# Halves of the expert weights made two tiles ahead, and unread products in bursts of eight, in a float32 Mamba-2 and mixture-of-experts block

## The chip, the core and the metric

The kernel runs on one core of a Trainium2 chip. The metric is the device time of one execution in microseconds (us), the median of several runs. Engines are named as the profile names them: PE is TensorE's matmul side and PEld its weight loads, DVE is VectorE, ACT is ScalarE, POOL is GpSimd, SP is SyncE, which here only starts DMAs.

## The reference

The input is 4 sequences of 512 tokens with 256 features in float32, so 2048 tokens. A modulated layer norm feeds a Mamba-2 style attention part (64 heads), whose result is added to the input. A second modulated layer norm feeds a mixture of experts, whose result is added again. The part that matters here is the routed experts:

```python
probs = softmax(x @ gate_w.T)                    # 64 experts
topk_w, topk_idx = top_k(probs, 6)               # 6 experts per token
topk_w = topk_w / sum(topk_w)
h = silu(einsum('th,eih->tei', x, experts_w1))   # inner size 176
y = einsum('tei,ehi->teh', h, experts_w2)
routed_out = einsum('teh,te->th', y, combine)
```

The reference computes all experts for all tokens and keeps six of them. The kernel computes only the pairs that were chosen.

## The kernel before

The program has four stages: the attention part, the second norm with routing, the two shared experts, and the routed experts. During routing each token's row is sent by indirect DMA into a region of its expert in the DRAM tensor `grouped`. The routed work is then a list of ETILES = 160 tiles of 128 rows (2048 * 6 / 128 + 64); each tile has one expert, and the tables `owner_no` and `first_row` in SBUF give its number and its first row. Tiles beyond the used ones run on a spare row region. After the last tile a stage of 16 groups (`got`, lines 386 and 1291 on) gathers six rows per token, scales them with the token's shares and adds them to the result.

Every float32 product is made of three products of halves: `split_mm` (lines 400 to 402) multiplies high by high, high by low and low by high. The high half is a rounded copy made by ScalarE (`high`, line 718) in the type fp32r, the low half is the difference, made by VectorE (`low`, line 888). Both helpers serve many tiles, so the rows are told apart by the tile they write.

For tile i of the expert loop:

- SP loads 128 rows (`load_rows`, line 348, into `x_rows`, 12 buffers) and the expert's two weight matrices (`load_weights`, lines 337 and 339, into `ew`, DEEP = 4 buffers of 128 x 864). `load_weights(i)` waits until `w_lo` of tile i-4 has been made, which frees the buffer. Before every fourth tile `four` reads the next four row and expert numbers into SP's registers. Then SP issues, in this order: rows n, rows n+1, weights n, rows n+2, weights n+1, rows n+3, weights n+2, weights n+3.
- TensorE turns the rows with two transposes (`turn`, line 657) into `p_x`, two buffers. ScalarE makes `xe_hi` (in the trace `hw_hi`, 128x256) and VectorE `xe_lo` (`hw_lo`), both in `rows_in`.
- ScalarE makes `ew_hi` in `weights`, VectorE `ew_lo` in `weights_low`, 128x864 each. `weights(i)` waits for the load and for `second_mm` of tile i-4, `weights_low(i)` for `w_hi` of the same tile.
- `first` (twelve products of 128x128 with 88-column weights) waits for `w_lo` and `x_lo` of its tile and for `hid_silu` of tile i-2. ScalarE makes `hid` with Silu (line 876, `hid_rows`) and `hid_hi`, VectorE `hid_lo`.
- `second` (six products of 88x256) waits for `hid_lo` of its tile and `row_done` of tile i-2. VectorE copies the result (`row_done`, line 1264, `hsw`), and GpSimd sends it out with an indirect DMA (`scatter`, line 1368).
- `fill(n)` (line 687) issues n products of 128x512 into `bank[6]`, which nothing reads.

The order on each engine is written out by hand. TensorE, turn i: `turn(i+2)`, `first(i)`, `second(i-1)`, `fill(1)`; ahead of the loop `fill(24)`, `turn(0)`, `turn(1)`. ScalarE: ahead of the loop `weights(0)`, `rows_in(0)`, `rows_in(1)`; turn i: `weights(i+1)`, `rows_in(i+2)`, silu(i), `hid_hi`(i). VectorE: ahead of the loop `weights_low(0)`, `rows_in(0)`, `rows_in(1)`; turn i: `rows_in(i+2)`, `hid_lo`(i), `weights_low(i+1)`, `row_done(i-1)`. The semaphore counts of `START` are given at the beginning and stand in for work of tiles before the first.

Of the kernel before, what the change touches and what calls it, by code (L numbers as in the profile page):

```python
# [45 lines left out]
ETILES = (TOKENS * TOP_K) // P + EXPERTS  # L46
# [29 lines left out]
def program(nc, x_t, in_w, out_w, scalars, bc_w, bc_conv, dt_w, dt_bias, a_log, c_t, mod_w, gate_w, shared_w,  # L76
            shared_d, expert_w1, expert_w2, const, route_const, grouped, outputs, out_t):
    ctx = ExitStack()
    with ctx:
# [315 lines left out]
        def _(pe):  # L395
            mm = nc.tensor.matmul

            def split_mm(out, w_hi, w_lo, x_hi, x_lo, first, last):

                mm(out, w_hi, x_hi, start=first, stop=False)  # L400
                mm(out, w_hi, x_lo, start=False, stop=False)  # L401
                return mm(out, w_lo, x_hi, start=False, stop=last)  # L402
# [79 lines left out]
            for n in range(6 * KE):  # L482
                for k in range(KE):
                    i = mm(p_out[0][:, n * BATCH:(n + 1) * BATCH], modw[:, k, n * P:(n + 1) * P], cact[:, k, :],
                           start=k == 0, stop=k == KE - 1)
# [6 lines left out]
            with pe.Fori(0, BATCH) as b:  # L492
# [5 lines left out]
                for p, hi, lo, done in ((p_turn, dtw_hi, dtw_lo, "dt_mm"), (p_hid, bcw_hi[:, 0], bcw_lo[:, 0], "bc_mm"),  # L498
                                        (p_gate, bcw_hi[:, 1], bcw_lo[:, 1], "bc_mm")):
                    for k in range(KE):  # L500
                        i = split_mm(p[:, :], hi[:, k, :], lo[:, k, :], h_hi[:, k, x], h_lo[:, k, x],
                                     k == 0, k == KE - 1)
                    i.then_inc(S[done], 1)
                pe.wait_ge(S["dt_plus"], b + 1)
                for t in range(TILES):
                    i = nc.tensor.transpose(p_y[:, t * P:(t + 1) * P], dt_head[:, t * P:(t + 1) * P], ident)
                i.then_inc(S["dt_turned"], 1)
                with pe.Fori(0, TILES) as t:
                    for n in range(UNITS_PER_TILE):
# [4 lines left out]
                        for c in range(2):  # L514
# [11 lines left out]
                            for part_ in (at_hi, at_lo):  # L526
                                a = part_[:, :, :].rearrange("p t h -> p (t h)")[:, heads]
                                i = mm(bank[4 * (1 - n) + 2 + c][:, :], later_r, a[:, :, None].broadcast_to([P, HPU // 2, CHUNK]),
                                       start=False, stop=part_ is at_lo)
# [5 lines left out]
                for t in range(TILES):  # L535
                    i = mm(p_out[0][:, t * P:(t + 1) * P], bcf[:, 0, t * P:(t + 1) * P], bcf[:, 1, t * P:(t + 1) * P],
                           start=True, stop=True)
# [13 lines left out]
                for t in range(TILES):  # L551
                    i = mm(p_hid[:, 8 * t:8 * t + 8], ssq[:, t * P:(t + 1) * P], ones[:, 0:8], start=True, stop=True)
                i.then_inc(S["ssq_mm"], 1)
                pe.wait_ge(S["ssq_wide"], b + 1)
                for t in range(TILES):
                    i = mm(p_gate[:, t * P:(t + 1) * P], ones, rinv_diag[:, t * P:(t + 1) * P], start=True, stop=True)
# [4 lines left out]
            for b in range(BATCH):  # L561
                pe.wait_ge(S["normed_lo"], (BATCH + b + 1) * KE)
                for t in range(TILES):
                    g = b * TILES + t
                    x = slice(g * P, (g + 1) * P)
                    for k in range(KE):
                        i = split_mm(p_logit[g // 8][:, (g % 8) * EXPERTS:(g % 8 + 1) * EXPERTS], h_hi[:, k, x], h_lo[:, k, x],
                                     gatew_hi[:, k, :], gatew_lo[:, k, :], k == 0, k == KE - 1)
            i.then_inc(S["logit"], 1)

            for b in range(BATCH):
                if b >= 1:
                    pe.wait_ge(S["h_copied"], b)
                for t in range(TILES):
                    x = slice(b * SEQ + t * P, b * SEQ + (t + 1) * P)
                    for k in range(KE):
                        o = p_turned[t // 2][:, (t % 2) * EMB + k * P:(t % 2) * EMB + (k + 1) * P]
                        mm(o, h_hi[:, k, x], ident_r, start=True, stop=False)
                        i = mm(o, h_lo[:, k, x], ident_r, start=False, stop=True)
# [7 lines left out]
            for g in (7, 15):  # L587
                i = mm(p_count[:, P:P + EXPERTS], ones, sum8[:, g, :], start=g == 7, stop=g == 15)
            i.then_inc(S["count_mm"], 1)
            pe.wait_ge(S["earlier"], 3)  # L590
            for n in range(2):
                o = p_rank[n][:, :].rearrange("p (t e) -> p t e", t=8)
                mm(o, before_r[:, :], taken_r[:, 8 * n:8 * n + 8, :], start=True, stop=False)
                i = mm(o, ones[:, :], earlier[:, 8 * n:8 * n + 8, :], start=False, stop=True)
# [58 lines left out]
            def turn(i):  # L653
                pe.wait_ge(x_in[i % XD], 16 * (i // XD + 1))
                pe.wait_ge(S["x_lo"], START["x_lo"] + i - 1)
                for k in range(KE):
                    m_ = nc.tensor.transpose(p_x[i % 2][:, k * P:(k + 1) * P], x_rows[:, i % XD, k * P:(k + 1) * P], ident)
                m_.then_inc(S["x_turned"], 1)

            def first(i):  # L660
                r = i % DEEP
                pe.wait_ge(S["w_lo"], START["w_lo"] + i + 1)
                pe.wait_ge(S["hid_silu"], START["hid_silu"] + i - 1)
                pe.wait_ge(S["x_lo"], START["x_lo"] + i + 1)
                for a in range(2):
                    for k in range(KE):
                        w = slice(k * EXP_INNER + a * IHALF, k * EXP_INNER + (a + 1) * IHALF)
                        x = slice(k * P, (k + 1) * P)
                        m_ = split_mm(p_first[i % 2][0:IHALF, a * P:(a + 1) * P], ew_hi[:, r, w], ew_lo[:, r, w],
                                      xe_hi[:, r, x], xe_lo[:, r, x], k == 0, k == KE - 1)  # L670
                m_.then_inc(S["first_mm"], 1)
# [12 lines left out]
            def fill(times):  # L684

                for _ in range(times):
                    mm(bank[6][:, :], ident_r, h_hi[:, 0, 0:SEQ], start=True, stop=True)  # L687
# [7 lines left out]
            for i in range(ETILES):  # L695
                if i + 2 < ETILES:
                    turn(i + 2)
                first(i)
                if i:
                    second(i - 1)  # L700
                fill(1)
            second(ETILES - 1)

            for g in range(GTILES):
                pe.wait_ge(S["final"], START["final"] + KE * (g - 1))
                pe.wait_ge(S["acc_chain"], START["acc_chain"] + TOP_K * (g + 1))
                for k in range(KE):
                    i = nc.tensor.transpose(p_x[g % 2][:, k * P:(k + 1) * P], acc_rows[:, g % 2, k * P:(k + 1) * P], ident)  # L708
# [4 lines left out]
        def _(act):  # L713
            f = nc.scalar.activation

            def high(dst, src):

                return f(dst, src, ACT.Identity)  # L718
# [118 lines left out]
            for b in range(BATCH):  # L837
                act.wait_ge(S["h_turned"], b + 1)
                for n in range(2):
                    i = f(ht[:, b * TILES + 2 * n:b * TILES + 2 * n + 2, :], p_turned[n][:, :].rearrange("p (t n) -> p t n", t=2),  # L840
                          ACT.Identity)
# [14 lines left out]
            def weights(i):  # L856
                act.wait_ge(S[f"w_in{i % DEEP}"], 32 * (i // DEEP + 1))
                act.wait_ge(S["second_mm"], START["second_mm"] + i - 3)
                high(ew_hi[:, i % DEEP, :], ew[:, i % DEEP, :]).then_inc(S["w_hi"], 1)

            def rows_in(i):
                act.wait_ge(S["x_turned"], START["x_turned"] + i + 1)
                act.wait_ge(S["first_mm"], START["first_mm"] + i - 3)
                high(xe_hi[:, i % DEEP, :], p_x[i % 2][:, 0:EMB]).then_inc(S["x_hi"], 1)

            weights(0)
            rows_in(0)
            rows_in(1)
            for i in range(ETILES):
                if i + 1 < ETILES:  # L870
                    weights(i + 1)
                if i + 2 < ETILES:
                    rows_in(i + 2)
                act.wait_ge(S["hid_lo"], START["hid_lo"] + i - 1)
                act.wait_ge(S["first_mm"], START["first_mm"] + i + 1)
                f(hid[0:IHALF, i % 2, :], p_first[i % 2][0:IHALF, 0:2 * P], ACT.Silu).then_inc(S["hid_silu"], 1)  # L876
                act.wait_ge(S["second_mm"], START["second_mm"] + i - 1)
                act.wait_ge(S["hid_silu"], START["hid_silu"] + i + 1)
                high(hid_hi[0:IHALF, i % 2, :], hid[0:IHALF, i % 2, :]).then_inc(S["hid_hi"], 1)


        @block.vector
        def _(dve):
            v = nc.vector

            def low(dst, src, hi):

                return v.tensor_tensor(dst, src, hi.bitcast(F32), ALU.subtract)  # L888
# [231 lines left out]
            for n in range(2):  # L1120
                i = v.tensor_reduce(lmax[:, 8 * n:8 * n + 8], logits[n], AX_X, ALU.max)
# [9 lines left out]
            for t in range(GTILES):  # L1131
                i = v.max(top8[:, t, :], prob[:, t, :])
# [3 lines left out]
            for t in range(GTILES):  # L1136
                i = v.match_replace(rest[:, t, :], top8[:, t, :], prob[:, t, :], TINY)
# [49 lines left out]
            for n in range(2):  # L1187
                i = v.tensor_tensor(pos[:, 8 * n:8 * n + 8, :], region_of[:, None, :].broadcast_to([P, 8, EXPERTS]),
                                    p_rank[n][:, :].rearrange("p (t e) -> p t e", t=8), ALU.add)
            link(i)  # L1190
            link(v.scalar_tensor_tensor(key[:, :, :], pos[:, :, :], 1.0, taken_r[:, :, :].bitcast(F32), ALU.add, ALU.mult))
            for g in range(GTILES):
                i = v.max(key8[:, g, :], key[:, g, :])
# [58 lines left out]
            def rows_in(i):  # L1252
                dve.wait_ge(S["x_hi"], i + 1)
                low(xe_lo[:, i % DEEP, :], p_x[i % 2][:, 0:EMB], xe_hi[:, i % DEEP, :]).then_inc(S["x_lo"], 1)

            def weights_low(i):
                dve.wait_ge(S["w_hi"], i + 1)
                low(ew_lo[:, i % DEEP, :], ew[:, i % DEEP, :], ew_hi[:, i % DEEP, :]).then_inc(S["w_lo"], 1)

            def row_done(i):  # L1260
                dve.wait_ge(S["second_mm"], START["second_mm"] + i + 1)
                if i >= YD:
                    dve.wait_ge(row_out[i % YD], 16 * (i // YD))
                v.tensor_copy(y_rows[:, i % YD, :], p_row[i % 2][:, 0:EMB]).then_inc(S["row_done"], 1)  # L1264
# [4 lines left out]
            weights_low(0)  # L1269
            rows_in(0)  # L1270
            rows_in(1)
            for i in range(ETILES):
                if i + 2 < ETILES:
                    rows_in(i + 2)
                dve.wait_ge(S["hid_hi"], i + 1)
                low(hid_lo[0:IHALF, i % 2, :], hid[0:IHALF, i % 2, :], hid_hi[0:IHALF, i % 2, :]).then_inc(S["hid_lo"], 1)
                if i + 1 < ETILES:
                    weights_low(i + 1)
                if i:
                    row_done(i - 1)  # L1280
            row_done(ETILES - 1)


# [145 lines left out]
```

## Time and profile before

| What | us |
|---|---|
| median of three runs | 2077.67 |
| lowest and highest of them | 2066.0 and 2079.49 |
| the profiled execution | 2081.04 |
| its span, first to last instruction | 2079.3 |
| expert loop, window 1360.8 to 1998.5 of the span | 637.7 |

Of the span TensorE's matmuls are busy 79%, VectorE 65%, ScalarE 45%, GpSimd 32%. The mean granted TensorE clock is 0.842 of full speed.

How to read the rows: a row of the timeline has its start and its length in us, the engine, the line, the operation, the tile written and the tiles read (buffer numbers left out), and in brackets how long the engine was idle before it and what released it. "SPq" is a DMA issue on SP's queue. A row of the windows view has the window, its length, then busy us and instructions of each engine, the granted clock (PEclk), the mean busy share of the 16 DMA engines, and GB/s.

### The profile page before, as it was taken

The numbers are of one execution on the slowest core, as the hardware profiler recorded it, in microseconds if no ns is written. First come the engines' busy times: TensorE is split into PE (matmuls) and PEld (weight loads), VectorE is DVE, ScalarE is ACT, GpSimd is POOL, SyncE is SP. The second block draws the span as 40 slices with busy tenths as digits, with TensorE's granted clock in tenths as the row PEclk, the third lists the DMA queues.
The fourth block names the chain that finished last, engine by engine and source line by source line (L and its number), as shares of the span: only waits on it lengthen the run. The fifth ranks groups of instructions, "written<-read, shape, count | busy, mean of one in ns | idle before, by whom it ended". The sixth has DMA issues, their size and how long they took to land. (4 is left out here: it accounts for less than half of the span.)

```text
span 2079.3 us, 33315 instructions
## 1 busy us (share of the span) xinstructions
PE 1650.1 (79%) x9324; PEld 1240.9 (60%) x9324; DVE 1341.5 (65%) x2125; ACT 929.4 (45%) x1696; POOL 671.5 (32%) x554
## 2 busy tenths in 40 slices
PE   7689996899968999689997853289987966667741
PEld 5466664666646666466665742278876865556630
DVE  3578885788867888678885532644455455555547
ACT  3455554555545555455553201044444455555510
POOL 0334343343433443343440075612222222222210
PEclk8799998999989999899997575655577599999955
DMA  3011220122201212012210043254454455555434
GB/s 128 0 53 61 67 61 0 53 61 65 63 0 51 62 61 66 2 45 67 62 55 3 19 164 136 96 152 132 134 148 146 133 151 172 160 164 142 132 129 161
DMA packets 140945, 185.01 MB, mean 89 GB/s; under 512 B 19241, under 2 KB 113463, under 8 KB 140736
## 3 DMA queue, kind: packets, MB, share of 16 engines
q1 hardware_dynamic: 128576, 158.65, 25.7%
q0 software_dynamic: 12288, 25.41, 3.5%
q8 instruction: 35, 0.57, 0.1%
q14 instruction: 46, 0.38, 0.1%
HBM read 147.85 MB, written 44.50 MB: 93 GB/s over the span
## 5 line engine op out<-in xcount | busy, mean ns | idle before, releaser
L976 DVE SCALAR_TENSOR_TENSOR e<-bank,scal,e 128x511 f32<-128x511 f32 (+2 forms) x384 | 287.3, 748 | 52.6 <-ACT e L767 17.3
L1368 POOL DMA_INDIRECT outputs<-hsw,x_rows x160 | 157.5, 985 | 499.3 <-DVE hsw L1264 471.9
L1322 POOL TENSOR_TENSOR ssq<-ssq,ysq 128x512 f32<-128x512 f32 x128 | 164.4, 1284 | 466.2 <-ACT ysq L772 466.2
L400 PE MATMUL bank<-hw_hi,ew_hi 128*88 128x128 f32 x640 | 188.7, 298 | 135.6 <-DVE ew_lo L888 135.6
L888 DVE TENSOR_TENSOR hid_lo_rows<-hid_rows,hid_hi_rows 88x256 fp32r<-88x256 f32 x160 | 67.4, 421 | 306.1 <-ACT hid_hi_rows L718 210.8
L400 PE MATMUL bank<-h_hi,wi_hi 128*128 x512 | 240.2, 469 | 19.5 <-POOL wi_lo L1309 14.6
L475 PE MATMUL bank<-e,wn 128*128 128x512 f32 x512 | 252.9, 617 | 0.0
L400 PEld LDWEIGHTS bank<-hw_hi,ew_hi 128*88 128x88 f32 x640 | 125.5, 196 | 184.5 <-DVE ew_lo L888 184.5
L402 PE MATMUL bank<-h_hi,wi_lo 128*128 x512 | 204.0, 398 | 0.0
L401 PE MATMUL bank<-h_lo,wi_hi 128*128 x512 | 203.9, 398 | 0.0
L767 ACT ACTIVATE e<-bank,scal 128x512 f32<-128x512 f32 x128 | 99.7, 779 | 203.1 <-PE bank L402 203.1
L876 ACT ACTIVATE hid_rows<-bank 88x256 f32<-88x256 f32 x160 | 60.9, 381 | 285.8 <-PE bank L402 249.6
L1309 POOL TENSOR_TENSOR wi_lo<-wi,wi_hi 128x512 fp32r<-128x512 f32 x128 | 165.3, 1292 | 51.0 <-ACT wi_hi L718 51.0
L401 PE MATMUL bank<-hw_lo,ew_hi 128*88 128x128 f32 x640 | 180.2, 284 | 0.0
L402 PE MATMUL bank<-hw_hi,ew_lo 128*88 128x128 f32 x640 | 180.0, 284 | 0.0
L888 DVE TENSOR_TENSOR ew_lo<-ew,ew_hi 128x864 fp32r<-128x864 f32 x160 | 167.6, 1048 | 9.8 <-ACT ew_hi L718 9.8
L718 ACT ACTIVATE ew_hi<-ew 128x864 fp32r<-128x864 f32 x160 | 145.2, 908 | 43.1 <-DMA ew<-expert_w 43.1
L1011 DVE TENSOR_TENSOR m<-el,gmask 128x1024 f32<-128x1024 f32 x128 | 156.4, 1222 | 0.2
L400 PEld LDWEIGHTS bank<-h_hi,wi_hi 128*128 128x128 f32 x512 | 97.2, 190 | 87.5 <-issue 68.9
L779 ACT ACTIVATE e<-e 128x512 f32<-128x512 f32 x128 | 80.7, 630 | 152.8 <-DVE e L976 152.7
L1362 POOL DMA_INDIRECT grouped<-h_send,rows x96 | 100.4, 1046 | 140.1 <-DVE h_send L1205 97.3
L469 PE MATMUL bank<-m,xt 128*64 128x128 f32 x2048 | 140.1, 279 | 6.7 <-DVE xt L1017 6.7
(245 smaller groups left out, 3853.8 us busy)
## 6 DMA issues: line engine op xcount, KB each, us to landing
ew<-expert_w SPq DMA_DIRECT2D x320, 176.0 KB
wi<-in_w SPq DMA_DIRECT2D x128, 256.0 KB, 2.7
x_rows<-grouped SPq DMA_DIRECT2D x160, 130.0 KB
wo<-out_w SPq DMA_DIRECT2D x128, 128.0 KB, 2.3
got<-outputs SPq DMA_DIRECT2D x16, 768.0 KB, 4.3
grouped<-zeros_out SPq DMA_DIRECT2D x65, 130.0 KB
outputs<-hsw,x_rows POOLq DMA_INDIRECT x160, 3.0
x_all<-x_t SPq DMA_DIRECT2D x4, 512.0 KB, 8.5
```

The source lines that it names most:

```text
L400: mm(out, w_hi, x_hi, start=first, stop=False)
L401: mm(out, w_hi, x_lo, start=False, stop=False)
L402: return mm(out, w_lo, x_hi, start=False, stop=last)
L469: i = mm(p_y[head, t * P:(t + 1) * P], xt[:, t, head], m[:, t, hd, :], start=True, stop=True)
L475: i = mm(p_out[k][:, :], wn[:, par, k * P:(k + 1) * P], y[:, par, :], start=do_out == "first", stop=do_out == "last")
L718: return f(dst, src, ACT.Identity)
L888: return v.tensor_tensor(dst, src, hi.bitcast(F32), ALU.subtract)
L976: v.scalar_tensor_tensor(dst[:, d:], src[:, 0:SEQ - d], taps(TAPS - 1 - d), dst[:, d:], ALU.mult, ALU.add).then_inc(S[done], 1)
L1011: v.tensor_tensor(m[:, :, :, :].rearrange("p t h (r l) -> p (t h) r l", l=CHUNK), e[:, :, None, :].broadcast_to([P, TILES * 2, CPT, CHUNK] ...
L1309: return g_.tensor_tensor(dst, src, hi.bitcast(F32), ALU.subtract)
L1322: g_.tensor_tensor(ssq[:, :], ssq[:, :], ysq[:, :], ALU.add).then_inc(S["ssq_done"], 1)
L1368: g_.indirect_dma_start(outputs, bass.IndirectOffsetOnAxis(x_rows[:, i % XD, EMB:EMB + 1].bitcast(U32), 0), y_rows[:, i % YD, :], None, bo ...
```

## The change

ScalarE makes `weights(1)` ahead of the loop and in turn i, last of all, `weights(i+2)`. VectorE makes `weights_low(1)` ahead of the loop and in turn i `weights_low(i+2)` behind `row_done(i-1)`. TensorE issues `fill(8)` in turns 7, 15, 23 and so on, twenty times, in place of `fill(1)` in all 160. Loads, buffers and waits keep their code.

```diff
@@ TensorE
                 first(i)
                 if i:
                     second(i - 1)
-                fill(1)
+                if i % 8 == 7:
+                    fill(8)
             second(ETILES - 1)
@@ ScalarE
             weights(0)
             rows_in(0)
             rows_in(1)
+            weights(1)
             for i in range(ETILES):
-                if i + 1 < ETILES:
-                    weights(i + 1)
                 if i + 2 < ETILES:
                     rows_in(i + 2)
...
                 high(hid_hi[0:IHALF, i % 2, :], hid[0:IHALF, i % 2, :]).then_inc(S["hid_hi"], 1)
+                if i + 2 < ETILES:
+                    weights(i + 2)
@@ VectorE
             weights_low(0)
             rows_in(0)
             rows_in(1)
+            weights_low(1)
             for i in range(ETILES):
                 if i + 2 < ETILES:
                     rows_in(i + 2)
                 dve.wait_ge(S["hid_hi"], i + 1)
                 low(hid_lo[0:IHALF, i % 2, :], hid[0:IHALF, i % 2, :], hid_hi[0:IHALF, i % 2, :]).then_inc(S["hid_lo"], 1)
-                if i + 1 < ETILES:
-                    weights_low(i + 1)
                 if i:
                     row_done(i - 1)
+                if i + 2 < ETILES:
+                    weights_low(i + 2)
             row_done(ETILES - 1)
```

## Rows read from the trace of the kernel before

**Rows 1.** The tiles' view, ew_hi and hid_lo_rows: first and last product of the loop.

```profile
L400 PE MATMUL bank<-hw_hi,ew_hi x640: 238/293/410, 1360.8 to 1994.9; 128*88 128x128 f32 x160
...
L402 PE MATMUL bank<-ew_hi,hid_lo_rows x320: 278/285/418, 1365.7 to 1998.3; 88*128 88x256 f32 x160
```

**Rows 2.** Windows: a stretch at full clock, one at half, the whole loop.

```profile
1680.00:1880.00 200.00, 130.59 (x1155) 113.11 (x1155) 113.12 (x221) 103.46 (x221) 54.13 (x55) 1.00 0.56 164
1400.00:1500.00 100.00, 94.86 (x471) 82.02 (x471) 46.53 (x90) 43.89 (x88) 21.97 (x23) 0.50 0.45 131
1360.80:1998.50 637.70, 502.11 (x3356) 433.83 (x3354) 329.78 (x637) 306.34 (x637) 155.90 (x159) 0.77 0.49 142
```

**Rows 3.** Timeline of one tile at full clock, all engines.

```profile
1702.91 0.29 PE L400 MATMUL bank<-hw_hi,ew_hi 128*88 128x128 f32 x1 [1.25 <-DVE ew_lo L888]
...
1703.91 0.33 PE L400 MATMUL bank<-ew_hi,hid_hi_rows 88*128 88x256 f32 x1
...
1704.17 0.38 ACT L876 ACTIVATE hid_rows<-bank 88x256 f32<-88x256 f32 x1 [1.65 <-PE bank L402]
...
1704.64 0.42 ACT L718 ACTIVATE hid_hi_rows<-hid_rows 88x256 fp32r<-88x256 f32 x1
1704.69 0.39 PE L687 MATMUL bank<-h_hi,consts_r 128*128 128x512 f32 x1
1704.92 0.38 PE L657 MATMUL bank<-consts,x_rows 128*128 128x128 f32 x2
1704.96 0.91 ACT L718 ACTIVATE ew_hi<-ew 128x864 fp32r<-128x864 f32 x1
1705.09 0.42 DVE L888 TENSOR_TENSOR hid_lo_rows<-hid_rows,hid_hi_rows 88x256 fp32r<-88x256 f32 x1 [1.56 <-issue]
1705.43 1.05 DVE L888 TENSOR_TENSOR ew_lo<-ew,ew_hi 128x864 fp32r<-128x864 f32 x1
1705.78 0.36 ACT L718 ACTIVATE hw_hi<-bank 128x256 fp32r<-128x256 f32 x1
1706.40 0.41 DVE L1264 COPY hsw<-bank 128x256 f32<-128x256 f32 x1
1706.53 0.29 PE L400 MATMUL bank<-hw_hi,ew_hi 128*88 128x128 f32 x1 [1.23 <-DVE ew_lo L888]
...
1706.73 0.41 DVE L888 TENSOR_TENSOR hw_lo<-bank,hw_hi 128x256 fp32r<-128x256 f32 x1
```

**Rows 4.** Timeline of one tile at half clock, TensorE's products.

```profile
1444.57 0.41 PE L400 MATMUL bank<-hw_hi,ew_hi 128*88 128x128 f32 x1 [0.22 <-DVE ew_lo L888]
...
1446.39 0.52 PE L400 MATMUL bank<-ew_hi,hid_hi_rows 88*128 88x256 f32 x1
...
1447.77 0.63 PE L687 MATMUL bank<-h_hi,consts_r 128*128 128x512 f32 x1
1448.20 0.63 PE L657 MATMUL bank<-consts,x_rows 128*128 128x128 f32 x2
1449.05 0.41 PE L400 MATMUL bank<-hw_hi,ew_hi 128*88 128x128 f32 x1 [0.22 <-DVE ew_lo L888]
```

**Rows 5.** Timeline of SP's queue around the start of a group of four tiles.

```profile
1696.21 0.33 SPq L339 DMA_DIRECT2D ew<-expert_w  x1
1699.68 0.86 SPq L348 DMA_DIRECT2D x_rows<-grouped  x2
1700.72 0.33 SPq L337 DMA_DIRECT2D ew<-expert_w  x1
...
1701.70 0.34 SPq L348 DMA_DIRECT2D x_rows<-grouped  x1
```

**Rows 6.** The tile's view of x_rows: landing times of its loads.

```profile
DMA to landing us min/median/max: 2.1/3.0/4.6
```

**Rows 7.** Windows of 5 us: routing products, and the end of the 24 unread products.

```profile
1150.00:1155.00 5.00, 5.00 (x26) 5.00 (x25) 3.13 (x4) 4.38 (x6) 0.00 (x0) 0.50 0.00 0
...
1355.00:1360.00 5.00, 4.82 (x22) 3.71 (x20) 1.06 (x1) 1.28 (x3) 0.00 (x0) 0.92 0.82 232
```

## The prediction

> **What bounds the kernel now.** I read the page first (its slices show the two stages, attention and experts), then the tiles of the expert weights, windows over the expert loop, the timeline of one tile at each clock, and last the SP queue. The edit touches only the loop over 160 expert tiles. It lasts from 1360.8 to about 1998.5 us [rows 1], 637.7 us, 30% of the span, with a mean granted clock of 0.77 [rows 2]. The clock has two levels: 0.50 throughout 1400 to 1500 and 1.00 throughout 1680 to 1880 [rows 2]. A mean of 0.77 makes 54% of the loop full clock (2.4 GHz) and 46% half (1.2 GHz). A tile takes 1706.53 - 1702.91 = 3.62 us at full clock [rows 3] and 1449.05 - 1444.57 = 4.48 us at half [rows 4]. Check: 344/3.62 + 293/4.48 = 95 + 65 = 160 tiles.
>
> What ends a tile at full clock is a ring [rows 3]: the twelve products of first(i) start at 1702.91, silu at 1704.17, hid_hi at 1704.64, DVE's hid_lo at 1705.09, then on the same engine ew_lo at 1705.43 for 1.05 us, and first(i+1) at 1706.53, 50 ns after it. Before that TensorE is idle for 1.23 us, released by ew_lo. At half clock the same wait is only 0.22 us [rows 4], so there TensorE itself is nearly the bound. The reader should see that ew_lo is made one tile ahead but behind hid_lo, so that the next tile's first product hangs on this tile's last DVE work.
>
> **ScalarE's edit is none.** Its old order is weights(i+1), rows_in(i+2), silu(i), hid_hi(i); moving weights(i+2) to the end of turn i gives the same sequence of instructions. In the trace ew_hi already follows hid_hi at once (1704.64, then 1704.96) [rows 3]. Cost 0, nothing to hide.
>
> **VectorE.** ew_lo(i+2) goes behind row_done(i-1). No instruction is added: 160 each, same sizes. It now waits for ew_hi(i+2), which is ScalarE's newest product. Relative to silu (s = 0) [rows 3]: ew_hi starts at 0.79 and ends at 1.70; hid_lo starts at 0.92, the row copy at 1.26, and the engine would be free for ew_lo at 1.59. So ew_lo starts near 1.75 and ends near 2.8. Behind its wait stands xe_lo (to about 3.1), which first() needs two tiles later. The ring is cut: first(i+1) finds its ew_lo made during the turn before. VectorE per tile, start to start: 0.34 hid_lo, 0.33 copy, 0.97 ew_lo, 0.33 xe_lo = 1.97 us. ScalarE likewise: 0.47 + 0.32 + 0.82 + 0.36 = 1.97 us. These are no bounds if TensorE needs more.
>
> **TensorE.** From first to turn at full clock it issues 1704.92 - 1702.91 = 2.01 us, of which 0.23 is the unread product; the two transposes add 0.38 [rows 3]. Without the product a tile is 2.16 us, with one 2.39. The transposes may overlap the next product; then they cost as little as 0.23, and the tile without a product 2.01. I take 0.38, the record, and keep the other as a bound. The burst adds 8 x 0.23 = 1.84 us to every eighth tile; 20 x 8 = 160 products, as many as now, so the mean is (8 x 2.16 + 1.84)/8 = 2.39 us. Nothing reads the products, so behind a burst only the next turn and first wait; the other engines' queues run dry for 1.8 us, which costs nothing while TensorE is the bound. second(i-1) needs hid_lo(i-1), ready 1.34 us after silu, more than half a tile early.
> At half clock: 1448.20 - 1444.57 = 3.63 including 0.43 for the product, plus 0.63 for transposes [rows 4]: 3.83 us without, 4.26 on the average.
>
> **SP and the loads.** A load of ew waits for w_lo four tiles back, so it is released at about s + 2.8 of the tile six before it, and is needed by ew_hi four tiles after that, at + 0.8: about 4P - 2.0 for a period P. SP is slow: between 1696.54 and 1699.68 it fetches the next four row and expert numbers (3.14 us), two row loads take 1.04, a pair of weight loads 0.98 [rows 5]. Four tiles need 3.14 + 2 x 1.04 + 4 x 0.98 = 9.1 us, 2.28 per tile: under 2.39, but it comes in a lump. The first pair of a group is out only 0.98 + 3.14 + 1.04 + 0.98 = 6.1 us after the credit of the pair before it. The page gives no landing time for ew; row loads land in 2.1 to 4.6 us, median 3.0 [rows 6]. I take 4 us, as the DMA engines will be busier: now 0.56 of their time at 3.62 us a tile [rows 2], that is 2.03 us per tile, so 0.83 at 2.45. The load lands 2.8 + 6.1 + 4 = 12.9 us after the silu seven tiles back; ew_hi wants it 5P + 0.8 after that, 11.6 at P = 2.16, in groups with no burst in between. It is 1.3 us late. The silu behind it then comes 1.97 + 1.3 = 3.3 us after the last instead of 2.16, 1.1 late; its hid_lo is ready 1.34 us later, and second() would have taken it at 2.03, so TensorE stands for 0.4 to 0.5 us in eight tiles, 0.06 each. With a burst in between it is in time. Loads in 3 us cost nothing; loads in 6 us make P about 2.7. I take 2.45 us.
>
> **The clock** is worth as much as the ring. What raised it: 24 unread products back to back before the loop took it to a mean of 0.92 in 1355 to 1360 [rows 7]. What did not: 1150 to 1155, TensorE busy 5.00 of 5.00 us with 128-column weight loads around short products, stays at 0.50 [rows 7]. In the loop at half clock second (1.38 us) and the unread product (0.43) stand back to back, and it rises seldom; the burst makes this stretch 1.38 + 8 x 0.43 = 4.8 us without a pause or a transpose in it. At full clock the products' share grows, since 1.23 us of idleness goes, against 0.23 of product in seven tiles of eight. So I let the clock rise with the first burst, in tile 7, and hold.
> The Trainium skill (TensorE: Matmul & The Clock Gate, Part 1: The HAM clock gate) says that the clock is throttled by default and that sustained activity releases it; the rise under the 24 products agrees. By it alone the sum is the one below. Its Part 4 (PE-mode transpose) says that transposes don't count as activity like products, which speaks against taking the single product from beside them; no row here separates the two.
>
> **Sum.** Tiles 0 to 7 at half clock: 8 x 3.83 + 8 x 0.43 = 34 us. 152 x 2.45 = 372. Together 406 against 637.7: 231 us less. Outside the loop nothing changes. The profiled execution took 2081.04 us (span 2079.3), which gives 1850; it was 3.4 above the median of 2077.67, so the forecast is 1847.
>
> **Rivals.**
> 1. Supply: loads take 6 us or more, or SP's lumps add up. P = 3.0: 34 + 456 = 490, saving 148, 1930 us. For it: SP at 2.28 us a tile and the load engines at 0.82 in 1355 to 1360, when four tiles' weights come at once [rows 7]. Against it: four tiles of buffer, and SP can run ahead in row loads. 8%.
> 2. The clock stays as mixed as now, with 95 tiles at full and 65 at half: 95 x 2.45 + 65 x 4.26 = 510, saving 128, 1950 us. For it: it rises and falls repeatedly in the loop today, and seven tiles of eight lose their product. The skill's same page (A second HAM failure mode) describes small pauses between groups of products that make the clock swing. 14%.
> 3. The other side: the clock falls soon after each burst and the loop runs at half throughout, 160 x 4.26 = 682, 44 us longer, 2122. One mechanism, at the place where the single product was; it decides from 2.45x + 4.26(160 - x) = 637.7, so the kernel is slower if fewer than 24 tiles run at full clock. Against it: 95 do now with far more idleness. 4%.
> 4. The change does not do what it says: ew_lo is still what first() waits for, because ew_hi(i+2) comes late on ScalarE. Then nothing moves, 2078. Against it: ew_hi ends at 1.70, over 2 us ahead of first(i+2). 2%.
>
> **Numbers.** The forecast's own case, 72%, runs from P = 2.28 (SP's floor, overlapped transposes: 34 + 347, so 1821) to P = 2.7 (1885). The range reaches down to 1815 and up to 1945, which takes in the supply case and most of the mixed clock, and leaves out some 15%. A measurement here can tell about 1% from no change. Faster by over 1%: 72 + 8 + 14 = 94%; within: 2%; slower: 4%.
>
> **What would show it.** Right: TensorE's idle time before first(), released by ew_lo, all but gone; tiles 2.2 us apart and 4.0 at a burst; clock 1.00 from about 1400 to the end; ew_lo starting right behind the end of ew_hi; VectorE's wait for hid_hi short; load engines at 0.8. The supply step is wrong if ScalarE waits long for ew in every fourth or eighth tile; the clock step if windows of 0.50 recur after tile 7. The whole is wrong if first() still waits on ew_lo, or if the loop is longer than 500 us.

## The result and the profile after

The changed kernel takes 1838.11 us, the median of four executions (1831.92 to 1847.08), against 2078.58 for the kernel before on the same chip. The ratio is 0.8864 with a 95% interval of 0.8797 to 0.8931. The forecast was 1847 us. The profiled execution took 1831.92 us, with a span of 1830.1 us. Executions more than 1.5% above the fastest of their kernel are left out of every ratio and interval here and below but not of the medians, so a ratio can differ from the quotient of two medians; in group 3 below the ratios stand against 2042 and 2048 us alone.

The loop over the 160 expert tiles, from its first product to its last, in the tiles' view of the changed kernel. It answers to [rows 1]:

```profile
L400 PE MATMUL bank<-hw_hi,ew_hi x640: 238/242/305, 1358.2 to 1745.9; 128*88 128x128 f32 x160
...
L402 PE MATMUL bank<-ew_hi,hid_lo_rows x320: 274/282/292, 1361.3 to 1749.3; 88*128 88x256 f32 x160
```

The first product starts at 1358.2 and the last at 1749.3. The whole loop in the windows view, and a stretch inside it, to be read against [rows 2]:

```profile
1358.20:1749.50 391.30, 363.08 (x3356) 334.67 (x3355) 327.85 (x637) 301.87 (x637) 188.81 (x159) 1.00 0.82 231
1400.00:1700.00 300.00, 277.42 (x2571) 256.21 (x2571) 252.81 (x491) 232.87 (x492) 146.12 (x123) 1.00 0.84 240
```

The loop fell from 637.7 to 391.3 us, 246 us, which is the whole gain: the spans differ by 249. TensorE's clock is 1.00 all through it, in place of 0.77, and the DMA engines are busy 0.82 of the time in place of 0.49. VectorE and ScalarE did the same work (328 and 302 us against 330 and 306), so nothing became cheaper; the waits shrank.

Timeline of two tiles of the changed kernel, answering to [rows 3]. Line numbers of VectorE's and ScalarE's rows have moved by one or two:

```profile
1362.33 0.29 PE L400 MATMUL bank<-hw_hi,ew_hi 128*88 128x128 f32 x1 [0.20 <-DVE ew_lo L890]
...
1363.20 1.05 DVE L890 TENSOR_TENSOR ew_lo<-ew,ew_hi 128x864 fp32r<-128x864 f32 x1
...
1363.59 0.38 ACT L876 ACTIVATE hid_rows<-bank 88x256 f32<-88x256 f32 x1 [0.27 <-PE bank L402]
...
1364.06 0.42 ACT L719 ACTIVATE hid_hi_rows<-hid_rows 88x256 fp32r<-88x256 f32 x1
...
1364.09 0.38 PE L657 MATMUL bank<-consts,x_rows 128*128 128x128 f32 x2
...
1364.30 0.29 PE L400 MATMUL bank<-hw_hi,ew_hi 128*88 128x128 f32 x1
1364.38 0.91 ACT L719 ACTIVATE ew_hi<-ew 128x864 fp32r<-128x864 f32 x1
...
1364.51 0.42 DVE L890 TENSOR_TENSOR hid_lo_rows<-hid_rows,hid_hi_rows 88x256 fp32r<-88x256 f32 x1
...
1364.85 0.41 DVE L1266 COPY hsw<-bank 128x256 f32<-128x256 f32 x1
...
1365.32 1.06 DVE L890 TENSOR_TENSOR ew_lo<-ew,ew_hi 128x864 fp32r<-128x864 f32 x1
...
1366.44 0.29 PE L400 MATMUL bank<-hw_hi,ew_hi 128*88 128x128 f32 x1
```

The reader is to see three things. The tiles are 1.97 and 2.14 us apart where they were 3.62. Then, ew_lo starts at 1365.32, just behind the end of ew_hi (1364.38 + 0.91 = 1365.29): ScalarE's product is now what releases it, in the turn two tiles ahead of the one that needs it.

Last, the ring is not gone; it now spans two tiles. The product at 1366.44 is the first of the tile for which that ew_lo was made, and it starts 0.06 us after its end (1365.32 + 1.06 = 1366.38). The product at 1364.30 stands as close behind the ew_lo of its own tile (1363.20 + 1.05 = 1364.25). Its row has no bracket because the record of the transposes before it, 0.38 us long, covers the short wait. From the first product at 1362.33 it is 1.26 us to silu, 0.47 more to hid_hi, 0.32 to ew_hi, 0.94 to ew_lo and 1.12 to the first product two tiles on: 4.11 us for two tiles, 2.05 us for one. In 81 of the 159 tiles after the first one, the first product starts 0.05 to 0.06 us after the end of its ew_lo (in some of them ew_lo was late because its load was); in the kernel before it does so in all 159.

What still makes an engine wait, from the waits view between 1400 and 1740:

```profile
ACT ew_hi L719 <- DMA ew<-expert_w: 26.6, 37, 2.2
...
PEld bank L657 <- DMA x_rows<-grouped: 13.0, 21, 1.7
...
PEld bank L400 <- DVE ew_lo L890: 11.4, 15, 1.4
PE bank L657 <- DMA x_rows<-grouped: 7.8, 13, 1.5
PE bank L400 <- DVE ew_lo L890: 7.7, 13, 1.2
```

Columns are total us, times, longest us. Late loads, of weights and of rows, are the longest of these waits; the wait of `bank` for ew_lo holds late weights too. SP's own waits between 1360 and 1740, in the kernel before and in the changed one:

```profile
SPq L337 <- DVE ew_lo L888: 175.5, 67, 3.6
...
SPq L337 <- DVE ew_lo L890: 5.3, 8, 1.1
```

SP hardly waits for anything any more: it is busy nearly all of the time, and its queue shows why the loads are late. SP does not only start DMAs; it also reads the row and expert numbers of four tiles into its registers. Between two groups of four tiles there is the lump of [rows 5] again, here 1388.77 - (1384.86 + 0.32) = 3.6 us:

```profile
1384.86 0.32 SPq L339 DMA_DIRECT2D ew<-expert_w  x1
1388.77 0.43 SPq L348 DMA_DIRECT2D x_rows<-grouped  x2
1389.39 0.37 SPq L337 DMA_DIRECT2D ew<-expert_w  x1
```

### The profile page after: what moved, and what is told of

It is laid out like the page before. It is cut to its first block and busy times, and to the rows that moved or that the text cites. A ratio compares the mean times of both kernels' runs of the same rounds, so it can differ in the third digit from the quotient of the medians.

```text
span 1830.1 us, 33315 instructions
## 1 busy us (share of the span) xinstructions
PE 1511.1 (83%) x9324; PEld 1141.7 (62%) x9324; DVE 1339.1 (73%) x2125; ACT 924.9 (51%) x1696; POOL 704.3 (38%) x554
## 5 line engine op out<-in xcount | busy, mean ns | idle before, releaser
L1371 POOL DMA_INDIRECT outputs<-hsw,x_rows x160 | 190.1, 1188 | 220.0 <-DVE hsw L1266 182.4
L400 PE MATMUL bank<-hw_hi,ew_hi 128*88 128x128 f32 x640 | 160.6, 255 | 13.1 <-DVE ew_lo L890 9.4
L401 PE MATMUL bank<-hw_lo,ew_hi 128*88 128x128 f32 x640 | 151.5, 242 | 0.0
L402 PE MATMUL bank<-hw_hi,ew_lo 128*88 128x128 f32 x640 | 151.4, 242 | 0.0
L469 PEld LDWEIGHTS bank<-m,xt 128*64 128x64 f32 x2048 | 109.2, 136 | 53.2 <-issue 42.4
L475 PEld LDWEIGHTS bank<-e,wn 128*128 128x128 f32 x512 | 87.0, 189 | 84.5 <-issue 82.5
L1019 DVE TENSOR_TENSOR xt<-bank,dt 128x512 f32<-128x512 f32 x128 | 88.5, 691 | 55.5 <-PE bank L452 55.5
```

The lines of the kernel that those rows point to most:

```text
L469: i = mm(p_y[head, t * P:(t + 1) * P], xt[:, t, head], m[:, t, hd, :], start=True, stop=True)
L475: i = mm(p_out[k][:, :], wn[:, par, k * P:(k + 1) * P], y[:, par, :], start=do_out == "first", stop=do_out == "last")
L1371: g_.indirect_dma_start(outputs, bass.IndirectOffsetOnAxis(x_rows[:, i % XD, EMB:EMB + 1].bitcast(U32), 0), y_rows[:, i % YD, :], None, bo ...
```

## The experiments

The means per tile in this table are worked out from the timelines: start of the last silu row less start of the first, over 159. Kernels of one group ran on one chip. The part ahead of the loop differed by up to 24 us between the traces (1344 to 1368), most of it between chips, and the kernel before differs too, as its clock varies from execution to execution. Across groups the tile's mean is the better number.

| Group | Kernel | us (median) | Ratio to before, 95% | us per tile |
|---|---|---|---|---|
| 0 | changed | 1838 | 0.8864 (0.8797 to 0.8931) | 2.43 |
| 1 | before | 2039 | | |
| 1 | order alone, single products | 1815 | 0.8924 (0.8855 to 0.8994) | 2.42 |
| 1 | bursts alone, old order | 2113 | 1.0408 (1.0332 to 1.0484) | 4.25 |
| 1 | order, no unread products | 1882 (1852 to 1974) | none | 2.75 |
| 1 | changed, no bounds comparisons | 1795 | 0.8837 (0.8774 to 0.8901) | 2.28 |
| 2 | before | 2063 | | |
| 2 | changed, again | 1824 | 0.8863 (0.8763 to 0.8962) | 2.50 |
| 2 | old order, singles and bursts | 2033 | 0.9889 (0.9789 to 0.9988) | 3.74 |
| 2 | no comparisons, no unread products | 1785 (1777 to 1848) | 0.8658 (0.8541 to 0.8775) | 2.19 |
| 2 | changed, fewer bytes | 1813 | 0.8821 (0.8731 to 0.8910) | 2.36 |
| 3 | before | 2090 | | |
| 3 | no comparisons, single products | 1804 | 0.8816 (0.8718 to 0.8914) | 2.20 |
| 3 | no comparisons, one weight load | 1818 | 0.8880 (0.8832 to 0.8927) | 2.31 |
| 3 | before, no comparisons | 2078 (2047 to 2103) | none | 3.92 |
| 3 | no comparisons, bursts of four | 1804 | 0.8819 (0.8681 to 0.8956) | 2.23 |

**The order alone.** The changed kernel with the single product back:

```diff
-                if i % 8 == 7:
-                    fill(8)
+                fill(1)
```

> The two-ahead order with one unread product in every tile, as before the change. Theory A (the order alone gives the gain; any unread products are as good as bursts): the 24 products before the loop raise the clock, the tiles keep TensorE busy over 90% and it stays at 1.00; SP's queue still sets about 2.45 us a tile, so the loop is 385 to 400 us and the kernel within 1% of the changed one, 1830 to 1855. Theory B (the burst is what holds the clock): windows at 0.50 come back in the loop, tiles there take 4.1 to 4.3 us, the loop is 450 to 640 us and the kernel 1900 to 2080.

Theory A held: 1815 us and 2.42 us a tile, the same as the changed kernel. The clock was 1.00 but for one dip. Windows around it:

```profile
1460.00:1465.00 5.00, 3.70 (x33) 3.17 (x31) 3.10 (x8) 2.65 (x6) 1.98 (x2) 0.94 0.95 246
1465.00:1470.00 5.00, 5.00 (x30) 4.82 (x29) 3.73 (x7) 2.81 (x6) 2.73 (x2) 0.50 0.95 250
1470.00:1475.00 5.00, 5.00 (x29) 4.82 (x29) 2.21 (x5) 2.83 (x7) 1.12 (x1) 0.54 0.81 226
1475.00:1480.00 5.00, 5.00 (x51) 4.76 (x50) 4.62 (x10) 4.14 (x9) 2.20 (x2) 1.00 0.46 140
```

TensorE stands 1.3 us of five, the clock falls, and with the single products in each tile it is back ten us later. The order is the whole gain here; the burst was not needed for it.

**The bursts alone.** The kernel before with `fill(8)` in every eighth tile in place of `fill(1)` in all.

> The old one-ahead order with a burst of eight in every eighth tile. Theory A: the ring first, silu, hid_hi, hid_lo, ew_lo keeps 3.62 us at full clock; a burst tile adds 1.84 less its 1.23 us of idleness, 0.6. If the burst holds the clock at 1.00, the loop is 160 x 3.62 + 20 x 0.6 = 591 us, 46 less than before, the kernel about 2032. Theory B (clock worth nothing without the order, or falls between bursts): a mixed clock as before, loop 630 to 660, kernel 2070 to 2100.

Neither: it is 4.1% slower than the kernel before, and the loop, 682 us at a mean clock of 0.71, is longer than the 660 of theory B. One burst in the windows:

```profile
1375.00:1380.00 5.00, 4.35 (x26) 3.95 (x25) 2.06 (x4) 1.99 (x4) 1.50 (x2) 0.50 0.38 122
1380.00:1385.00 5.00, 5.00 (x21) 4.22 (x20) 1.72 (x3) 1.61 (x4) 1.15 (x2) 0.57 0.50 143
1385.00:1390.00 5.00, 3.24 (x35) 3.00 (x34) 2.48 (x5) 2.37 (x6) 0.32 (x1) 1.00 0.37 102
...
1400.00:1405.00 5.00, 3.62 (x30) 3.29 (x28) 2.14 (x5) 1.88 (x4) 1.83 (x2) 0.64 0.71 198
1405.00:1410.00 5.00, 4.35 (x24) 3.95 (x24) 2.06 (x4) 2.30 (x5) 1.11 (x2) 0.50 0.56 166
```

The clock rose at each of the twenty bursts, and after each but the last it was down again within two to seven tiles of 3.62 us (7 to 27 us), the tiles then 4.48 us. So the burst raises the clock and does not hold it, where the ring leaves TensorE idle in every tile.

**The order, and no unread products in the loop.** The two lines with `fill(8)` are gone.

> The two-ahead order with no unread product in the loop (the 24 before it stay). Theory A: TensorE is busy enough on its own, the clock stays at 1.00, and SP's queue (2.28 us a tile at least) and the loads set the pace: loop 365 to 392 us, kernel 1812 to 1838, so the bursts cost 0 to 1.4%. Theory B: without bursts the clock falls at the first longer wait for a load and stays at 0.50: tiles of 3.8 us, loop 500 to 610, kernel 1945 to 2055.

Between the two: 1852 to 1974 us in four executions, and a loop of 440 us in the profiled one. The clock fell three times, each time after TensorE had stood 1.3 to 1.4 us for an ew_lo, and it came back each time without any unread product, after 20, 137 and 31 us. The first fall, a stretch of the long one, and its end:

```profile
1365.00:1370.00 5.00, 5.00 (x53) 4.72 (x52) 4.77 (x11) 3.63 (x8) 2.83 (x3) 1.00 0.79 203
1370.00:1375.00 5.00, 3.39 (x28) 2.95 (x27) 3.10 (x6) 3.76 (x8) 1.46 (x2) 0.92 0.90 278
1375.00:1380.00 5.00, 5.00 (x32) 4.98 (x31) 4.20 (x10) 3.19 (x6) 2.20 (x3) 0.50 0.94 262
...
1500.00:1520.00 20.00, 20.00 (x115) 20.00 (x114) 11.99 (x23) 10.82 (x23) 6.83 (x6) 0.50 0.64 180
...
1585.00:1590.00 5.00, 4.96 (x48) 4.73 (x48) 3.62 (x9) 3.72 (x8) 2.32 (x2) 0.91 0.70 211
```

In the row from 1500 TensorE's matmul and weight-load records are both busy 20.00 of 20.00 us, at half clock, 3.53 us a tile. The Trainium skill (TensorE: Matmul & The Clock Gate, Part 1) has sustained activity release the throttle; here TensorE's records leave no gap for 38 tiles, and the clock stays at 0.50 all that time before it rises. What raised it at 1586 these runs do not show. Nor does a wait of this length always lower it: the changed kernel stood 2.03 us before 1650.9, and its clock stayed at 1.00.

**Less work on SP.** The changed kernel, where the reads of row and expert numbers carry no comparison with their bounds:

```diff
-                                                                min_val=0, max_val=top)[1]
+                                                                min_val=0, max_val=top,
+                                                                skip_runtime_bounds_check_because="clamped by the routing")[1]
```

> The changed kernel, in which SP reads row and expert numbers without comparing each with its bounds (eight comparisons in every fourth tile less; nothing computed is left out). Theory S (SP's queue is the bound behind the ring): the lump between two groups falls from 3.3 us to some 2 us, SP's floor from 2.28 to 2.0 us a tile, TensorE's waits for row loads and ScalarE's for weight loads shrink, the loop goes from 391 to 365-380, kernel 1815 to 1828. Theory D (the load engines, busy 0.84, are the bound): the loop stays within 5 us of 391.

Theory S held: 2.28 us a tile, the loop 366 us against 391. The kernel's 1795 us is below the expected 1815, as its loop begins 13 us earlier than in group 0 (1345.0 and 1358.2). The lump, on SP's queue of this kernel:

```profile
1506.95 0.34 SPq L339 DMA_DIRECT2D ew<-expert_w  x1
1508.65 0.85 SPq L348 DMA_DIRECT2D x_rows<-grouped  x2
1509.69 1.31 SPq L337 DMA_DIRECT2D ew<-expert_w  x1
```

It is 1508.65 - 1507.29 = 1.4 us where it was 3.1 to 3.6. In the windows view TensorE is busy 295.90 of 300 us, with the DMA engines at 0.89:

```profile
1400.00:1700.00 300.00, 295.90 (x2762) 274.64 (x2761) 268.16 (x525) 247.33 (x526) 151.85 (x131) 1.00 0.89 253
```

Undisturbed tiles are now the rule: 1.87 to 2.23 us apart from silu to silu, mean 2.04, and 3.75 to 4.03 with a burst. What sets them is the ring over two tiles: in 112 of 159 tiles the first product starts within 0.06 us of the end of its ew_lo. TensorE's own time for a tile can be read behind a burst, when ew_lo has long been ready (for the product at 1475.73 it ended at 1474.12):

```profile
1471.84 2.00 PE L688 MATMUL bank<-h_hi,consts_r 128*128 128x512 f32 x8
...
1473.68 0.38 PE L658 MATMUL bank<-consts,x_rows 128*128 128x128 f32 x2
1473.82 0.30 PE L401 MATMUL bank<-hw_hi,ew_hi 128*88 128x128 f32 x1
...
1475.73 0.30 PE L401 MATMUL bank<-hw_hi,ew_hi 128*88 128x128 f32 x1
```

The burst takes 1473.68 - 1471.84 = 1.84 us, the two transposes hold the next product up by 0.14 though their record is 0.38 long, and a tile is 1475.73 - 1473.82 = 1.91 us. The other 0.14 us of the 2.05 are waiting for ew_lo.

This version beats the kernel before and the order-alone version of its group; the changed kernel ran in the other groups, at 1824 and 1838 us.

**The changed kernel again**, in group 2.

> The changed kernel itself, beside the experiments of this group on one chip. Theory A (single products hold the clock as well as bursts once the order is cut): 1810 to 1825, within 1% of the order-alone version. Theory B (the burst adds something of its own): below 1800.

1824 us: theory A. Its trace shows what the group-0 trace did not: two falls of the clock, each at a wait of 1.3 us of TensorE for an ew_lo whose load was late, and each ended by the next burst. The first of them:

```profile
1505.00:1510.00 5.00, 3.67 (x34) 3.33 (x34) 3.50 (x8) 3.25 (x7) 2.04 (x2) 0.95 0.85 218
1510.00:1515.00 5.00, 5.00 (x31) 5.00 (x31) 3.80 (x7) 2.91 (x7) 2.44 (x2) 0.50 0.82 224
...
1520.00:1525.00 5.00, 5.00 (x23) 4.52 (x23) 3.24 (x5) 2.00 (x4) 1.81 (x2) 0.50 0.62 175
1525.00:1530.00 5.00, 5.00 (x41) 4.53 (x40) 1.33 (x4) 2.18 (x6) 0.43 (x1) 0.84 0.65 184
```

Both falls lasted 17 us, where the three of the kernel without unread products lasted 20, 137 and 31 us and the one of the kernel with single products 10 us. So a burst can bring the clock back; that it limits a fall to eight tiles rests on these two. They also explain why this trace has 2.50 us a tile and that of group 0, at full clock throughout, 2.43.

**Old order, single products and bursts.**

```diff
-                fill(1)
+                fill(8 if i % 8 == 7 else 1)
```

> The old one-ahead order with the single product in every tile and seven more in every eighth. Theory A (the burst raises the clock, the single product or equal work in each tile holds it, so the burst-alone version lost by the missing singles): clock 1.00 in nearly the whole loop, 3.62 us a tile and 0.6 us more at a burst, loop 590 to 605 us, kernel 2025 to 2040. Theory B (in the old order the clock falls after a burst whatever stands in the other tiles): a mixed clock near 0.7, loop 660 to 680, kernel 2095 to 2120.

Theory A: 2033 us, and a clock of 0.95 between 1400 and 1900, with five falls in the loop, the longest of seven tiles. The burst raises the clock and the single product in each tile helps to hold it: without the singles it was soon down again after every burst but the last. The gain over the kernel before is 1.1% with an interval of 0.1 to 2.1%, so at the edge of what can be told. A burst tile takes 3.75 us, 0.13 more than the others and not 0.6: in this order TensorE needs 1.91 + 0.23 = 2.14 of 3.62 us, and seven more products (1.61 us) fill the 1.48 that it stands.

```profile
1400.00:1900.00 500.00, 363.14 (x2943) 316.12 (x2943) 277.43 (x536) 255.28 (x537) 132.30 (x135) 0.95 0.55 156
```

**No comparisons and no unread products.**

> Two-ahead order, no bounds comparisons on SP, no unread product in the loop. Theory A (the clock fell without unread products only because SP's lumps made TensorE stand still): with the lumps gone the clock holds at 1.00, a tile takes 2.05 us, the loop is 330 to 345 us, kernel 1760 to 1780. Theory B (the clock needs the unread products whatever the supply): it falls to 0.50 for long stretches at 3.53 us a tile, loop 400 to 560, kernel 1830 to 1990.

In between. The clock held in the profiled execution (1.00 in the whole loop, in which TensorE never stood longer than 0.91 us), and the median is 1785 us, the lowest of all; by the tile it is level with the single products below (2.20). But one execution of four took 1848 at a mean clock of 0.860 against 0.898 to 0.905. A tile takes 2.19 us and not 2.05: the DMA engines are at 0.92, and ScalarE waits for weights again.

```profile
1400.00:1700.00 300.00, 281.52 (x2719) 259.18 (x2718) 278.65 (x544) 256.36 (x543) 162.59 (x138) 1.00 0.92 257
```

**Fewer bytes.** The second weight load brings one of its two halves, so half of each second matrix is left out of the result.

```diff
-                sp.dma_start(ew[0:IHALF, i % DEEP, W1_COLS:ECOLS].rearrange("p (h n) -> p h n", h=2),
-                             expert_w2[bass.ds(e, 1), :, :, :].rearrange("a h p n -> p (a h) n"))\
+                sp.dma_start(ew[0:IHALF, i % DEEP, W1_COLS:W1_COLS + EMB],
+                             expert_w2[bass.ds(e, 1), 0, :, :].rearrange("a p n -> p (a n)"))\
...
-            v.memset(ew[P // 2:P, :, W1_COLS:ECOLS], 0.0).then_inc(S["zeros_set"], 1)
+            v.memset(ew[:, :, W1_COLS:ECOLS], 0.0).then_inc(S["zeros_set"], 1)
```

> The changed kernel, in which the second half of each expert's second matrix is not loaded (its place holds zeros), so 90 KB of some 590 KB a tile less are moved, with the same number of DMA issues on SP. Theory S (SP's issue of DMAs and register reads is the bound): the loop stays at 380 to 392 us. Theory D (the load engines' time is the bound): it follows the bytes, 15% less, 330 to 355 us.

Theory S, mostly: 2.36 us a tile against the 2.43 of group 0, 3% for 15% fewer bytes, though the DMA engines' share fell to 0.70 from 0.84 there. (The 2.50 and 0.81 of its own group hold the two falls of the clock.) Taking 2 us of SP's time in every fourth tile gave more than taking 90 KB from every tile.

**No comparisons, single products.**

> Two-ahead order, no bounds comparisons on SP, one unread product in every tile in place of the bursts. Theory A (with the supply in time TensorE's own work is the bound and 160 unread products cost the same wherever they stand): 2.28 us a tile, loop 360 to 368, kernel 1790 to 1800, the same as with bursts within 0.5%. Theory B (the burst has a value or a cost of its own): a difference over 0.7%.

Theory B, in favour of the single product: 2.20 us a tile against 2.28 with bursts, 0.07 x 160 = 12 us in the loop. The kernel's 1804 us holds 20 us more ahead of the loop, which began at 1365.0 and not at 1345. Its undisturbed tiles are 2.13 to 2.15 us apart, 0.10 above the 2.04 without a product:

```profile
1402.41 1.06 DVE L890 TENSOR_TENSOR ew_lo<-ew,ew_hi 128x864 fp32r<-128x864 f32 x1
...
1403.33 0.40 PE L688 MATMUL bank<-h_hi,consts_r 128*128 128x512 f32 x1
1403.56 0.38 PE L658 MATMUL bank<-consts,x_rows 128*128 128x128 f32 x2
1403.69 0.30 PE L401 MATMUL bank<-hw_hi,ew_hi 128*88 128x128 f32 x1
...
1405.46 0.40 PE L688 MATMUL bank<-h_hi,consts_r 128*128 128x512 f32 x1
```

The product still takes 0.23 us of TensorE (1403.33 to 1403.56). But the first product at 1403.69 comes 0.22 us after the end of its ew_lo (1403.47), so here TensorE's own work sets the tile: 1.91 + 0.23 = 2.14. Without the product TensorE had 1.91 us of work and 0.14 of waiting in the ring. Spread out, a product fills that wait and costs 0.10; the 1.84 us of a burst come at one place and are paid nearly whole (2.04 + 1.84/8 = 2.27, and 2.28 measured).

**No comparisons, one weight load per tile.** `load_weights` makes one DMA of 128 x 864 from matrices that lie side by side, with zeros for the 40 missing rows; ScalarE's wait then counts one load in place of two.

```diff
-                sp.dma_start(ew[:, i % DEEP, 0:W1_COLS], expert_w1[bass.ds(e, 1), :, :].rearrange("a p n -> p (a n)"))\
-                    .then_inc(S[f"w_in{i % DEEP}"], 16)
-                sp.dma_start(ew[0:IHALF, i % DEEP, W1_COLS:ECOLS].rearrange("p (h n) -> p h n", h=2),
-                             expert_w2[bass.ds(e, 1), :, :, :].rearrange("a h p n -> p (a h) n"))\
+                sp.dma_start(ew[:, i % DEEP, :], expert_w[bass.ds(e, 1), :, :].rearrange("a p n -> p (a n)"))\
                     .then_inc(S[f"w_in{i % DEEP}"], 16)
```

> No bounds comparisons, bursts kept, and each expert's two matrices laid side by side in memory with the missing 40 rows as zeros, so that one DMA per tile brings both: one issue of 0.45 us less on SP, 128 long pieces in place of 304 short ones, but 442 KB in place of 360. Theory S (issues on SP are what is left of the supply bound): SP floor 1.5 us a tile, stalls gone, loop 360 to 364. Theory D (the load engines go by bytes; they are busy 0.89 already): 2.3 to 2.4 us a tile, loop 368 to 385, kernel 1800 to 1817. If they go by pieces, their share falls well below 0.89.

No gain: 2.31 us a tile. The engines moved 289 GB/s at a share of 0.91:

```profile
1400.00:1700.00 300.00, 293.05 (x2715) 271.11 (x2715) 265.16 (x517) 242.94 (x518) 146.37 (x130) 1.00 0.91 289
```

That is 0.91 x 2.31 = 2.10 us of their time per tile against 0.89 x 2.28 = 2.03 with two loads: 16% more bytes (289 x 2.31 against 253 x 2.28) for 3 to 4% more time. They go neither by bytes alone nor by pieces alone. SP was already out of the way: without the comparisons it waited 61 us for ew_lo between 1360 and 1700, and with one load 72, where in the changed kernel it was 5. What set the tile in both is the ring and the bursts, 2.27 us.

**The kernel before, no comparisons.**

> The kernel before the change, without the bounds comparisons on SP. Theory S: SP had idle time there (it waited for ew_lo), so the same edit that takes 29 us off the changed kernel takes nothing in the loop; a few us at most in routing; within 1% of before, apart from the clock's share. Rival (the comparisons delay something in both): 1.5% or more faster.

The tiles are 3.62 and 4.48 us apart as before, so the edit that takes 25 us off the changed loop does nothing in the old one. The kernel's time says little, 2047 to 2103 beside 2042 to 2105 for the kernel before: the clock's share moves it more than 1%.

**No comparisons, bursts of four.**

> Two-ahead order, no bounds comparisons, bursts of four in every eighth tile in place of eight. Theory A (unread products are paid in full once TensorE is the bound, and half as many still bring the clock back after a fall): 20 x 4 x 0.21 = 17 us less than with eight, 1775 to 1785, and no run with long stretches at half clock. Theory B (the load engines take over as the bound at once): less than 8 us gained, 1787 or more.

Theory B: 2.23 us a tile against 2.28, 0.04 x 160 = 6 us and not 17. With less TensorE work the loads show: the DMA engines are at 0.91, and TensorE is busy 286.63 of 300 us where it was 295.90.

## Why the prediction was right

The outcome was right, 1838 us against 1847. The steps behind it were in part wrong, and the nearness is in part luck.

The ring: its wait went as forecast, its end did not. TensorE's wait for ew_lo before first(), by the page 135.6 us in its matmul row before, is 9.4 now, and ew_lo starts right behind ew_hi, at 1.73 us after silu, and ends at 2.79, as worked out. But the ring is not cut; it spans two tiles and allows one tile in 2.05 us. The prediction's own figures hold this bound. ew_lo(i+2) ends 2.8 us after silu(i), and first(i+2) comes 2P - 1.26 after it, so P cannot fall below (2.8 + 0.05 + 1.26)/2 = 2.06. The step saw no bound there because it took 2.16 for TensorE.

TensorE's tile: mis-sized. The transposes cost 0.14 us, less than the 0.38 taken and less than the 0.23 of the lower bound. So TensorE needs 1.91 us and not 2.16 or 2.01. That undisturbed tiles are 2.04 us apart, close to that lower bound, is the ring's doing and luck for the forecast. The burst costs the 1.84 us that were taken. The single product takes 0.23 us of TensorE too, but adds only 0.10 to a tile.

The supply: the right mechanism, mis-sized. The step gave 0.06 us of stall per tile. Measured: 2.43 - (2.04 + 1.84/8) = 0.16. What it left out is that the row loads come late too; "SP can run ahead in row loads" does not hold when SP never waits. This error and that of TensorE's tile cancel, so 2.45 us a tile was forecast and 2.43 measured: luck again. SP as the cause is shown by the kernel without comparisons; the kernel with fewer bytes shows the DMA engines as a smaller second. Rival 1 was thus present in small size.

The clock: the outcome was right, the start was not. The step let the clock stay at 0.50 until the first burst and took 34 us for eight tiles. It never fell; those tiles took 18.6 us, and that is the 15 us between the 406 us forecast for the loop and the 391 measured. In the kernel before, it fell after TensorE had stood 1.96 us before its second tile; that wait was the ring's. The rise was put down to the burst, and in the profiled execution no burst was needed for it. That it holds because the idleness goes is borne out by the single products with one fall of 10 us, and by the kernel with neither comparisons nor unread products with none in its trace. With SP's lumps and no unread products it fell three times, so the new order alone did not hold it there. "Worth as much as the ring" is true in one sense only: 160 tiles of the old order at full clock would take 579 us, so at most 58 of the 246 us can come from the clock; but a tile of the new order at half clock takes 3.53 us, or 3.96 with a product, and would have left almost nothing of the ring's gain.

The rivals: rival 2 did not happen in the profiled execution and happened in small in the next (two falls of five tiles). The text has the range up to 1945 take in most of it, but its own figure is 1950, outside. Rival 3, the clock down soon after each burst, is what the bursts do without the new order, at 4.1% slower, though at a mean clock of 0.71 and not at 0.50 throughout. Rival 4 was dismissed too easily. Its condition, first() still waiting for ew_lo, holds in 81 of 159 tiles, and ew_hi(i+2) ends 2 x 2.16 - 1.26 - 1.70 = 1.36 us ahead of first(i+2) and not over 2. What did not follow is that nothing moves, because the ring now pays for two tiles at once. "The whole is wrong if first() still waits on ew_lo" was too sharp a sign for the same reason.

The rest: nothing outside the loop changed (246 of 249 us).

## What to carry to other kernels

Making an operand one turn earlier does not cut a ring of waits; it lets the ring span one tile more. Add up its links again, divide by the number of tiles, and compare with each engine's own work: here 4.11/2 = 2.05 us against TensorE's 1.91. A short wait can hide behind a long record, so compare the start of the waiting instruction with the end of what it waits for.

Look next at the queue that feeds the ring: here SP, with 2.28 us of issuing and register reads per tile, was hidden behind 3.62 us and kept the pace at 2.43. Try the cheap work there first: leaving out eight comparisons in every four tiles was worth 25 us of 391. Unread products belong where they fill existing idleness, one at a time; a burst in one place was paid nearly whole.

## What was not expected of the hardware

Eight register values read and compared with their bounds took SP 3.1 to 3.6 us; without the comparisons 1.4 us. TensorE's records can be busy 20.00 of 20.00 us with the clock at 0.50 and stay so for over 100 us, and the clock can then rise without any unread product. Two transposes with a record of 0.38 us held the next product up by 0.14 us. Padding 360 KB in 304 pieces to 442 KB in 128 pieces raised the DMA engines' time per tile only from 2.03 to 2.10 us.
